# A two-layer decoder on one Trainium2 core: in the second layer's attention, `values` goes ahead of `scores`, and ScalarE's `by_key` behind its exponents

## The reference

```python
q = (x @ Wq.T).reshape(b, t, 8, 64)
kv_latent = x @ Wkv_down.T                      # 64 wide
k = (kv_latent @ Wk_up.T).reshape(b, t, 8, 64)
v = (kv_latent @ Wv_up.T).reshape(b, t, 8, 64)
scores = jnp.einsum('bqhd,bkhd->bhqk', q, k) * scale
attn = jax.nn.softmax(scores, axis=-1)
out = jnp.einsum('bhqk,bkhd->bqhd', attn, v).reshape(b, t, 512)
x = x + out @ Wo.T
...
x = x + cross_attention(layernorm(x), ctx)      # one head, 77 keys, masked
x = x + quantised_feed_forward(layernorm(x))
```

## Time and profile before

| | |
|---|---|
| median of 3 runs | 1689.8 us (1682.85 to 1690.56) |
| profiled execution | 1675.36 us, its span 1673.6 us |
| mean granted clock of TensorE | 0.968 of full speed |
| TensorE busy | 1536.0 us, 92% of the span |
| VectorE, ScalarE, GpSimd busy | 979.0, 842.2, 468.4 us |

### The profile page before, as it was taken

The page is one execution under the profiler, slowest core; times in us unless marked ns, Lnnn a source line. Parts: engine busy times, 40 slices in busy tenths (PEclk is TensorE's granted clock), DMA queues, the critical chain, the costliest instruction groups (busy, mean ns, idle before and its releaser), DMA issues. The chain is left out here.

```text
span 1673.6 us, 27432 instructions
## 1 busy us (share of the span) xinstructions
PE 1536.0 (92%) x10279; PEld 1083.3 (65%) x10279; DVE 979.0 (58%) x2296; ACT 842.2 (50%) x1849; POOL 468.4 (28%) x592
## 2 busy tenths in 40 slices
PE   8999999998987899999999899999999989996299
PEld 5676767766755777787777466666666654442288
DVE  3665766767766435222222567766664568777883
ACT  4446555555555422211212565666656533597980
POOL 4223234253234410000002665555542300032100
PEclk9999999999998999999999999999999889998599
DMA  3440111011151154334424211110100000000031
GB/s 115 156 156 18 47 30 44 30 47 44 34 165 39 61 164 137 125 113 126 153 87 136 70 39 52 43 34 27 39 14 14 1 25 1 0 1 15 24 99 65
DMA packets 100929, 108.32 MB, mean 65 GB/s; under 512 B 25410, under 2 KB 89804, under 8 KB 100800
## 3 DMA queue, kind: packets, MB, share of 16 engines
q1 hardware_dynamic: 94656, 90.01, 17.3%
q0 software_dynamic: 6144, 16.57, 3.1%
HBM read 64.77 MB, written 42.01 MB: 64 GB/s over the span
## 5 line engine op out<-in xcount | busy, mean ns | idle before, releaser
L1795 POOL TENSOR_SCALAR c_pr<-c_pr,c_rsum 128x256 f32<-128x256 f32 x256 | 128.2, 518 | 190.2 <-DVE c_rsum L2211 189.8
L2089 ACT ACTIVATE c_pr<-bank,c_nmax 128x256 f32<-128x256 f32 x256 | 118.0, 473 | 119.9 <-DVE c_nmax L2206 119.8
L1526 ACT ACTIVATE b_G<-bank 128x320 f32<-128x320 f32 x128 | 56.0, 437 | 210.8 <-PE bank L1475 210.8
L1475 PE MATMUL bank<-b_XT,shared 128*128 128x320 f32 x512 | 154.6, 437 | 0.0
L2206 DVE TENSOR_REDUCE c_nmax<-bank 128x2 f32<-128x512 f32 x128 | 82.4, 685 | 108.6 <-PE bank L1854 108.5
L1489 PE MATMUL bank<-shared,b_G 128*128 128x256 f32 x640 | 142.2, 379 | 0.0
L1489 PEld LDWEIGHTS bank<-shared,b_G 128*128 128x128 f32 x640 | 120.9, 190 | 17.8
L1072 DVE TENSOR_TENSOR hT_all<-bank,a_causal 128x512 f32<-128x512 f32 x128 | 79.4, 682 | 67.5 <-PE bank L563 67.5
L498 POOL TENSOR_TENSOR a_L<-a_L,a_Lm 128x1232 f32<-128x1232 f32 x32 | 72.0, 2249 | 149.5 <-DVE a_Lm L1087 149.5
L1475 PEld LDWEIGHTS bank<-b_XT,shared 128*128 128x128 f32 x512 | 92.5, 193 | 27.6 <-issue 1.2
L1545 DVE COPY b_Y<-bank 128x256 f32<-128x256 f32 x80 | 33.9, 424 | 120.3 <-PE bank L1489 120.1
(11 more groups left out here) (376 smaller groups left out, 3400.2 us busy)
## 6 DMA issues: line engine op xcount, KB each, us to landing
shared<-L_ffn_w SPq DMA_DIRECT2D x32, 512.0 KB, 6.0
t_slots_in<-a_h SPq DMA_DIRECT2D x20, 512.0 KB, 7.5
shared<-t_slots_in SPq DMA_DIRECT2D x15, 640.0 KB, 7.3
t_slots_out<-b_Y SPq DMA_DIRECT2D x15, 640.0 KB, 4.1
hT_all<-x SPq DMA_DIRECT2D x8, 512.0 KB, 4.0
a_xr<-x SPq DMA_DIRECT2D x8, 512.0 KB, 3.9
t_x_a<-a_x SPq DMA_DIRECT2D x8, 512.0 KB, 2.9
shared<-t_x_a SPq DMA_DIRECT2D x8, 512.0 KB, 4.3
```

The costliest lines, as they stand in the source:

```text
L1475: t = p.matmul(P[2 + n % 2][:, 0:HC], w1[e % 3][:, u, 128 * f:128 * f + 128], XT[e % 2][:, u, HC * m:HC * m + HC], start=(u == 0), stop=(u ...
L1795: p.tensor_scalar(pr[k][:, e, u, :], pr[k][:, e, u, :], rsum[k][:, e, u:u + 1], 1.0, ALU.mult, ALU.mult).then_inc(q.pr_ready, 1)
L2089: a.activation(pr[t % 2][:, e, u, :], P[e][:, S * u:S * u + S], ACT.Exp, bias=nmax[t % 2][:, e, u:u + 1], accum_out=sums[t % 2][:, e, u:u ...
```

## The change

On TensorE `values(t - 2)` moves from behind `turn(t - 1)` to ahead of `scores(t)`. On ScalarE `heads(t - 2)` moves from behind the exponents to ahead of them, and `by_key(t - 1)` from behind the slot's copies for other work to straight behind the exponents. In the tail, `values(TAIL - 2)` moves in the same way.

```diff
@@ tensor, for t in range(TAIL)
+                    if t >= 2:
+                        values(t - 2)
                     scores(t)
                     if t == 0:
                         queries(0, 1)
                         queries(0, 2)
                     if t >= 1:
                         turn(t - 1)
-                    if t >= 2:
-                        values(t - 2)
                     if s == 0 and late:
                         x_turn(g - 2)
@@ tensor, tail
+                values(TAIL - 2)
                 scores(TAIL)
                 turn(TAIL - 1)
-                values(TAIL - 2)
                 project(Z, 0)
@@ scalar, for t in range(TAIL)
+                    if t >= 2:
+                        heads(t - 2)
                     exponents(t)
+                    if t >= 1:
+                        by_key(t - 1)
                     if t in (0, 1):
                         keep_unit(f"q{t + 2}", 0, qT[0][:, t + 2, :], bank(f"q{t + 2}", 0)[:, :])
-                    if t >= 2:
-                        heads(t - 2)
...
                     if s == 6 and ahead:
                         keep_unit("q2", g + 1, qT[(g + 1) % 2][:, 2, :], bank("q2", g + 1)[:, :])
-                    if t >= 1:
-                        by_key(t - 1)
```

## The result

| | before | changed |
|---|---|---|
| median, 6 runs each | 1685.06 us | 1716.68 us (1714.19 to 1719.67) |
| ratio | | 1.0184, 95% interval 1.0163 to 1.0206 |
| profiled execution, span | 1673.6 us | 1712.5 us |
| mean granted clock | 0.968 | 0.964 |

The change makes the kernel slower by 1.8%, 31.6 us between the medians. I forecast +38 us on a median of 1689.8, that of the three runs I had then.

A forecast was written before the change was run, and what follows sets the result against it. TensorE was taken to bound the second layer, busy 49.4 of 51.7 us a group. Waits of +27 us and clock falls of +11 gave +38 on the 1689.8 us median: 1728 us, 8-in-10 range 1702 to 1750.

The forecast's parts named there:

- The floor (step 2): TensorE, values ahead of scores: values must wait for by_key, so no slot can be shorter than 5.46 us.
- The lost cover (step 3): TensorE's other work starts 1.01 us earlier, its ScalarE copies come 0.2 later: up to 1.2 us more waiting.
- ScalarE's part (step 1): ScalarE: heads ahead of exponents costs nothing, hidden behind scores; by_key straight behind them removes 2.3 us of turn's waits.
- The sum: Slot changes add to 3.6 us per full group; with waits and clock, +38 us in all.
- the waits alone: Second layer's added waits: 18 us in five full groups, 9 in the other three, +27 us, bounds 12 and 33.
- The clock term: TensorE's clock falls once a group in seven groups, from new idle stretches, 1.6 us each: +11 us.
- new stretches like these arise in s=1, s=4 and s=6: TensorE idle in these slots, 1.8, 1.4 and 1.4 us, could bring its clock down.
- the sign that I named: Profile of the changed kernel: granted clock should show one stretch under 1.00 in most groups.
- A: Rival, faster: turn's waits (10.0+2.3 us) go and the new floor is hidden, 1678 us; chance 5%.
- B: Rival, no change: later copies cost nothing since TensorE's idle moves, not grows, 1690 us; chance 7%.
- C: Rival: clock falls at each of three places in every group, 38 us on top of 27, 1755 us; chance 15%.
- D: Rival: waits only and the clock stays, 1717 us; chance 25%.

The follow-up runs named there:

- ahead_s6: Kernel before, with values(t-2) ahead of scores and heads(t-2) ahead of the exponents only in slots s=6: 1.0078 times before.
- scalar_only: Kernel before, with only ScalarE's new order (heads ahead of the exponents, by_key straight behind them), TensorE's order unchanged: 1.0425 times before.
- the filled variant: The full change plus filler transposes ahead of values in s=1, in first- and last-group gaps, and ahead of x_scores in every group: 1.0133 times before, 1711.85 us.
- after_dve_bykey_first: The full change, with VectorE's half of by_key ahead of the added context in s=1: 1.0144 times before.
- after_filled: The full change plus filler transposes ahead of values in s=1 and in the first and last groups' long gaps, s=6 mostly unfilled: 1.0140 times before.
- between: Kernel before, with values(t-2) moved only one step earlier, between scores(t) and turn(t-1), ScalarE as before: 0.9921 times before.

## Why the prediction was right, point by point

**The floor (step 2) held.** Predicted slot lengths against measured: s=1 5.96 and 6.12, s=3 5.46 and 5.40. The differences are the time from the end of a copy to the matmul behind it: 0.26 us for VectorE's in s=1, where I had 0.11, and 0.06 for ScalarE's in s=3 (1118.85+0.60 to 1119.51), where I had 0.14. Behind s=1 the gain of s=2 was foreseen too (-1.31, measured -1.52), and that it would be eaten. That the pair gave +0.48 where I had +0.53 is partly luck: s=1 came out 0.16 longer and s=2 0.2 shorter than predicted. That `values` would wait some 10 us in all was too low: 20.5, since the first and the last group have slots with nothing else in them, and there the floor bites most (up to 2.95 us).

**The lost cover (step 3) held.** s=0 +0.64 (predicted +0.62), s=4 +0.11 (+0.18), s=5 +0.58 (+0.55), s=6 +1.23 (+1.24). `ahead_s6` shows it alone.

**ScalarE's part (step 1) held**, and needed its cover: `scalar_only` shows what `heads` costs without it.

**The sum.** A full group rose by 3.24 us where I had 3.6. The 0.36 between them is s=2 and s=7, 0.2 us each, which I had at 6.76 and 6.75 and which last 6.56. With the clock kept up the layer is 415.4 us, of which 0.8 are the fillers' own. The falls that the kernel before already had cost about 2.2 us (worked out below), so the waits alone cost some 415.4-0.8-(392.4-2.2)=24.4 us, where I had +27: 16 for my 18 in the five full groups, 8.3 for my 9 in the other three (1.2, 2.7 and 4.4 for 3 each).

The forecast of 1728 lies 11 us above the measured 1716.7. Of these 4.7 are the median of the kernel before, which six runs put at 1685.06 and my three at 1689.8, and 6.4 are the loss, 31.6 for 38.

**The clock term was mis-sized.** I took one fall a group, seven in all, at 1.6 us each: 11 us. The price of one was right (a full group of 56.61 us for 55.02), the count was not. The two profiles of the change have five and four falls in the layer. Against the filled variant they cost 7.5 and 6.6 us, or 8.3 and 7.4 with the fillers' own 0.8, and 4 to 5 of that is the last group's. The kernel before had two falls already, which the prediction left out of its sum, although show the second. They cost some 2.2 us in its last group: half of `turn` 0.89 us from start to start for 0.58, values 1.91 for 1.01, `project` 4.03 for 3.65, `x_scores` 2.50 for 1.91. Net 5 to 6 for 11. The step that was mis-sized is "new stretches like these arise in s=1, s=4 and s=6": the gap in s=6, six times in each execution, passed without a fall in the two profiles of the change and in that of `after_dve_bykey_first`, and brought two in that of `after_filled`; the one in s=4 brought none in any; those of s=1 brought one in each profile of the change. So the sign that I named, a stretch under 1.00 in most groups, was there in one of the five full groups.

**The rivals.** A needed `by_key` 1.3 us earlier; it came where the rows had it. B (later copies cost nothing) is out by s=3, s=5 and s=6, which grew by 0.39, 0.58 and 1.23 us. C is out: most gaps bring no fall. D, 1717 with the waits alone, is nearest to the measured 1716.7, but by luck: it puts 27 us of waits on a median of 1689.8, and the runs show some 24 us of waits and 6 of clock on 1685.1.

The Trainium skill ("TensorE: Matmul & The Clock Gate", section "HAM oscillation — how this bites in real kernels") tells of a fall in each turn of a loop whose waits are about 3 to 5 us long. The prediction set that loop equal to rival C, whose gaps are 1.4 to 1.8 us, and that was not the same case. The one gap here of such a length, 3.25 us in the last group, had a fall behind it in both profiles of the change, so there the trace agrees. Of the shorter ones the wait of 0.95 us brought none in any of five groups, those of about 1.5 us brought one in some executions and not in others.

## What to carry to other kernels

Where an in-order engine must wait, what stands between the wait and its releaser matters more than where the wait is: `values` one place earlier gained 0.8%, two places earlier lost 3.0%, or 1.8% with ScalarE's order changed to suit. Before moving a step ahead, list both what it will wait for and what it used to cover; here the second list cost more than the first in each full group. An isolated gain (the wait for GpSimd was wholly removed) is to be read together with its neighbours: count from scores to scores over a whole period, not by the wait that goes.

## What the runs showed of the hardware

- The order of matmuls alone changes TensorE's time by up to 0.2 us a slot, with no wait. In s=7 the same scores, turn, values and `project` take 6.75 us when `values` stand directly ahead of `project`, and 6.55 to 6.56 when `turn` does (in the change, in `between`). `project` shows 3.62 us for 3.72, and starts 0.93 us after turn's start where it starts 1.01 after values'. In `between` this is 0.76 us of the 1.77 that a full group gained. I did not test why.
- The same gap in the same code lets the clock fall in one execution and not in the next. One fall made a full group 56.61 us long for 55.02. Filling gaps with useless transposes made the layer 6.65 us shorter.
